# Layer norms of a four-layer block kernel: application and turn moved, their bank changed, constants loaded by another queue

## What is computed

```python
x = x + jnp.tanh(g_xattn[l]) * attention_l(_layernorm(x), ctx_4096, ...)
x = x + jnp.tanh(g_ffn[l]) * ffn_l(_layernorm(x), ...)

def _layernorm(x, axis=-1, eps=1e-05):
    m = jnp.mean(x, axis=axis, keepdims=True)
    v = jnp.var(x, axis=axis, keepdims=True)
    return (x - m) / jnp.sqrt(v + eps)
```

## Time and profile before

| | us |
|---|---|
| median of 3 runs | 2834.5 |
| lowest and highest | 2828.12 and 2834.67 |
| profiled execution, its own time | 2834.56 |
| its span in the trace | 2832.7 |
| PE busy | 2510.4 (89%) |
| DVE busy | 1857.0 (66%) |
| ACT busy | 1303.8 (46%) |
| POOL busy | 1286.5 (45%) |

### The profile page before, as it was taken

One profiled execution on the slowest core, in us unless ns is written; L12 is line 12 of the kernel. 1 busy time (PEld: TensorE's weight loads), 2 busy tenths in 40 slices (PEclk: granted clock), 3 DMA queues, 4 the chain that ended last, 5 costly groups with the idle time before them and its releaser, 6 DMA issues.

```text
span 2832.7 us, 42470 instructions
## 1 busy us (share of the span) xinstructions
PE 2510.4 (89%) x13827; PEld 2123.7 (75%) x13827; DVE 1857.0 (66%) x3455; ACT 1303.8 (46%) x3752; POOL 1286.5 (45%) x1423
## 2 busy tenths in 40 slices
PE   4899999997899999999978886878589999999865
PEld 3788888886778888888757775655468888888643
DVE  4777777767677777776757663522467777776765
ACT  2454545453245555555435443123145555555323
POOL 4554545543234444444436553334344444444245
PEclk7999999998899999999999997899799999999878
DMA  3111111111012222212000002269211111110047
GB/s 116 48 33 35 35 39 35 35 33 34 12 53 79 97 94 88 69 35 68 31 8 8 5 10 66 67 227 303 67 34 48 34 38 34 36 33 12 8 161 255
DMA packets 69102, 178.95 MB, mean 63 GB/s; under 512 B 10515, under 2 KB 11217, under 8 KB 66682
## 3 DMA queue, kind: packets, MB, share of 16 engines
q1 hardware_dynamic: 52048, 112.25, 12.3%
q0 software_dynamic: 13632, 61.10, 6.5%
q10 hardware_dynamic: 3210, 2.89, 0.3%
HBM read 157.84 MB, written 37.25 MB: 69 GB/s over the span
## 4 chain that ended last, share of the span: by engine, by line
PE 74%; DVE 8%; DMA 6%; issue 5%; POOL 5%; ACT 3%; ACTq 0%; POOLq 0%; SPq 0%; DVEq 0%
PE B_qkv L670 28%; PE B_out L670 19%; PE B_oT L741 4%; PE B_s L721 4%; PE B_qT L711 3%; PE B_oT L670 3%; PE B_pt L731 2%; PE B_s L722 1%; DMA raw<-in_experts,tables 1%; DMA raw<-slots_y,tables 1%; PE B_s L670 1%; PE B_oT L808 1%; PE B_qT L670 1%; POOL ring_l L1939 1%; PE B_qT L907 1%
## 5 line engine op out<-in xcount | busy, mean ns | idle before, releaser
L1179 ACT ACTIVATE W<-S,nmx 128x128 f32<-128x128 f32 x768 | 297.7, 394 | 58.2 <-DVE nmx L1469 58.2
L1947 POOL TENSOR_SCALAR rn<-ss 128x5 f32<-128x5 f32 x128 | 25.7, 201 | 621.5 <-DVE ss L1412 621.5
L1076 ACT ACTIVATE sq<-B_qkv 128x640 f32<-128x640 f32 x128 | 90.3, 706 | 423.7 <-PE B_qkv L670 423.7
L1968 POOL TENSOR_TENSOR S<-S,mask 128x512 f32<-128x512 f32 x192 | 251.5, 1310 | 17.0 <-ACT S L1019 16.9
L1487 DVE SCALAR_TENSOR_TENSOR X<-B_out,gates,X 128x512 f32<-128x512 f32 x200 | 150.1, 751 | 164.6 <-PE B_out L670 163.2
L2007 POOL TENSOR_TENSOR W<-W,rden 128x512 f32<-128x512 f32 x192 | 200.4, 1044 | 105.9 <-DVE rden L1474 105.8
L670 PE MATMUL B_qkv<-ring_h,xnT_h 128*128 128x512 f32 x512 | 216.3, 422 | 5.0 <-DVE xnT_l L1321 5.0
L670 PE MATMUL B_out<-ring_h,oT_h 128*128 128x512 f32 x516 | 209.6, 406 | 12.3 <-DVE kT L1459 8.6
L721 PE MATMUL B_s<-kT,qT_h 128*128 128x256 f32 x768 | 203.4, 342 | 11.0 <-DVE xnT_l L1321 9.8
L670 PE MATMUL B_out<-ring_l,oT_h 128*128 128x512 f32 x516 | 209.3, 406 | 0.1
L670 PE MATMUL B_out<-ring_h,oT_l 128*128 128x512 f32 x516 | 208.7, 404 | 0.0
(11 more groups left out here) (452 smaller groups left out, 8179.8 us busy)
## 6 DMA issues: line engine op xcount, KB each, us to landing
raw<-in_pieces SPq DMA_DIRECT2D x270, 256.0 KB
slots_y<-S SPq DMA_DIRECT2D x31, 256.0 KB
slots_y<-y SPq DMA_DIRECT2D x15, 256.0 KB, 8.2
X<-in_x ACTq DMA_DIRECT2D x8, 256.0 KB, 3.1
raw<-in_ctxT SPq DMA_DIRECT2D x8, 256.0 KB
rows_x<-xn SPq DMA_DIRECT2D x8, 256.0 KB, 2.0
out_x<-X SPq DMA_DIRECT2D x8, 256.0 KB, 3.3
raw<-in_quant SPq DMA_DIRECT2D x4, 256.0 KB
```

Of the source, the lines that this page charges most:

```text
L1179: t = act.activation(W[:, k, cols(r)], S[:, k, cols(r)], ACT.Exp, bias=nmx[:, k, r:r + 1], accum_out=den[:, k, r:r + 1])
L1968: pool.tensor_tensor(S3, S3, m.unsqueeze(1).to_broadcast([P, R, P]), ALU.add).then_inc(*masked.now((layer, u)))
```

## The change

norm spreads over two iterations: stats at place 12 of iteration i, apply at place 6 of i+1 (was 37 of i), turn at place 45 of i+1 for ffn0, ffn1 and ffn3 and at 33 for attention (was 7). The turns of the feed-forward stages go to bank B_oT instead of B_sc. The loads of X stand at iteration (b-2)//2: b=1 to 3 in iteration 0, 4 and 5 in 1, 6 and 7 in 2. The 12 small loads go from ACT to SP: gates in iteration 3, the other ten one at a time in iterations 14 to 23. The tanh stands in iteration 5 and DVE's make_constants in 28, both at place 57; the bias lands in the xn buffer instead of W.

```diff
-    def norm(self, i, stage, b, late=False):
+    def norm(self, i, stage, b):
         self.at(i, 12, "ln_stats", stage, b)
-        self.at(i, 37, "ln_apply", stage, b)
-        self.at(i + 1, 66 if late else 7, "ln_turn", stage, b)
+        self.at(i + 1, 6, "ln_apply", stage, b)
+        self.at(i + 1, 45 if stage.startswith("ffn") else 33, "ln_turn", stage, b)
...
         for b in range(1, NB):
-            self.at(max(0, b - 2), 1, "load_x", b)
+            self.at(max(0, (b - 2) // 2), 1, "load_x", b)
...
-        self.at(1, 2, "late_constants")
-        self.at(2, 5, "make_constants")
+        for n in range(CONSTANTS):
+            self.at(3 if n < 2 else 12 + n, 1, "load_constant", n)
+        self.at(5, 57, "make_gates")
+        self.at(16 + CONSTANTS, 57, "make_constants")
...
-            return (B_qT, "qT") if (stage, b) in plan.between or stage in ("attn0", "attn1", "attn3") else (B_sc, "sc")
+            return (B_qT, "qT") if (stage, b) in plan.between or stage in ("attn0", "attn1", "attn3") else (B_oT[:, :], "oT")
...
-            def make_constants():
+            def make_gates():
                 act.wait_ge(*small["g_xattn"].of(0))
                 act.wait_ge(*small["g_ffn"].of(0))
                 act.activation(gates[:, :], gates[:, :], ACT.Tanh).then_inc(*tanhed.now(0))
-                W_reader[0] = const.of("bias_hi"), const.of("bias_lo")
...
-                biases = W[0:LO_ROW + E3 + 1, 0, :]
+                biases = xn[0:LO_ROW + E3 + 1, 0, :]
...
+            def load_constant(n):
+                name, dst, src = (("g_xattn", gates[:, 0:4], io["g_xattn"].partition_broadcast(P)),
...
+                if name == "bias":
+                    for b in range(NB - 2, NB):
+                        sync.wait_ge(*ln_turned.of(("attn0", b)))
+                sync.dma_start(dst, src).then_inc(*small[name].now(0))
```

More of the change, by code:

```diff
@@ L42 @@
 VSLOTS = 6
+CONSTANTS = 12
 CHUNKS = NB * 2 * R
@@ L1025, in load_small @@
                 act.dma_start(dst, src).then_inc(*small[name].now(0))
-            def rows(vec):
-                return vec.partition_broadcast(P)
             def prologue():
@@ L1309, in scalar_program @@
             parts = {"project2": project2, "turn_q2": turn_q2, "exp2": exp2, "turn_p2": turn_p2, "oT2": copy_o2,
-                     "load_x": load_x, "late_constants": late_constants, "make_constants": make_constants, "ln_turn": ln_turn,
+                     "load_x": load_x, "make_gates": make_gates, "ln_turn": ln_turn,
                      "split": split, "project": project, "turn_q": turn_q, "split_k": split_k, "scores": scores, "low_scores": low_scores, "exp": exp, "turn_p": turn_p, "times_v": times_v, "low": low,
@@ L2138, in load @@
                     sync.dma_start(raw[:, k, :], io["pieces"][row][:, part]).then_inc(*landed[k].now(i))
+            def load_constant(n):
+                name, dst, src = (("g_xattn", gates[:, 0:4], io["g_xattn"].partition_broadcast(P)),
+                                  ("g_ffn", gates[:, 4:8], io["g_ffn"].partition_broadcast(P)),
+                                  ("bias", xn[0:LO_ROW + E3 + 1, 0, :], io["bias"]),
+                                  ("mask13", mask13[:, :], io["mask13"]),
+                                  ("mask2", mask2u[:, :].bitcast(I32), io["mask2"]),
+                                  *((f"norm_w{k}", norm_w[:, k:k + 1], io["norm_w"][k]) for k in range(4)),
+                                  ("groupmask", groupmask[:, :], io["groupmask"]),
+                                  ("gate_b", gate_b[:, :], io["gate_b"].partition_broadcast(P)),
+                                  ("rev", rev[:, :], io["rev"].partition_broadcast(P)))[n]
+                if name == "bias":
+                    for b in range(NB - 2, NB):
+                        sync.wait_ge(*ln_turned.of(("attn0", b)))
+                sync.dma_start(dst, src).then_inc(*small[name].now(0))
             def fill_tables():
@@ L2177, in tile3 @@
                 sync.dma_start(slots_y[t * P:(t + 1) * P, :], y3[:, t % 4, :]).then_inc(*y_stored[t % 4].now(t))
-            parts = {"load": load, "fill_tables": fill_tables, "clear_slots": clear_slots,
+            parts = {"load": load, "load_constant": load_constant, "fill_tables": fill_tables, "clear_slots": clear_slots,
                      "keep_rows2": keep_rows2, "fill_dispatch2": fill_dispatch2, "turn_ids2": turn_ids2, "contract2": contract2,
```

## The result

| | before | after |
|---|---|---|
| median, us | 2832.2 (4 runs) | 2922.2 (4 runs) |
| lowest and highest | 2828.12 and 2834.67 | 2918.37 and 2926.24 |
| span of the profiled execution | 2832.7 | 2920.8 |
| mean granted clock | 0.945 | 0.925 |

The change costs 90 us: ratio 1.0319, 95% interval 1.0299 to 1.0340. The forecast was 2902, the range 2855 to 2932.

The account below looks back on a forecast made before the run. The prediction took PE, busy 89% of the span, as the bound, so its waits are mostly paid in full. From 2834.6 us, +62.3 of waits and +5 of slower clock gave 2902, range 2855 to 2932.

Parts of the forecast that it names:

- The sum of the waits: All stages: the start's gain and the later turns' waits on PE, together +62.3 us.
- Start: said -3: Kernel start: ACT's 12 load issues go, so the first copies and turn_q come sooner; -3 us, bounds -6 and +2.
- ffn0 and attn1 together: said 32.4: Iterations 64 to 75: xnT_l comes later and PE waits for it; +23.6 us for ffn0, +8.8 for 72 to 75.
- ffn1: said 7.5: ffn1's iterations: the product waits for the later turn, copy and xnT_l; +7.5 us, bounds 2 and 14.
- attn3: said 6.6: attn3: first projection and last two turns later, other turns absorbed by additions of gathered rows; +6.6 us, bounds 2 and 14.
- ffn3: said 18.8: ffn3: the turn waits for the bias addition in B_oT, so route3 starts later; +18.8 us, bounds 8 and 26.
- The clock: PE's granted clock, lowered by more waits: 24 us possible in ffn0, ffn3 and ffn1, only 5 taken.
- rival (a): ffn0, ffn1 and ffn3: the full 24 us of slower clock comes due, giving 2921 us; chance 0.16.
- (b): All iterations: DVE sets the pace; freed of 46.3 us of waits it has xnT_l ready in time, 2812 us; chance 0.08.
- (c): Waits swap one for one, as in attn3: 2834 us, the same time; chance 0.04.
- (d): Half the bank waits are covered by work the forecast put in series: 2850 us; chance 0.08.
- The +14: Some 15 steady iterations would pay 0.95 us each if applications met POOL's work at the new place; left to the range.

Follow-up runs that it names:

- turn_mid: Kernel before with the change's start and the turn moved to place 33 (attention) and 36 (ffn), application left at 37, old banks: ratio 1.0207, 2887.8 us.
- const_only: Kernel before with only the small constant loads moved to SyncE one at a time and finished later, X loads as before: 2827.4 us, ratio 0.9994.
- the filling: The whole change plus unread small matmuls while PE waits, ahead of turns in ffn0 and ffn1 and of ffn1's products, in two bank versions: 2931.7 and 2930.4 us.
- apply_late: Kernel before with the change's start and the application at place 55 of its old iteration instead of 37, turns at 7: 2823.1 us, ratio 0.9974.
- start_only: Kernel before with only the change's start (constant loads and earlier X loads), norms and banks as before: 2825.3 us, ratio 0.9975.
- apply_only: Kernel before with the change's start and the application at place 6 of the next iteration, turn still at 7, old banks: ratio 1.0213.
- turn36_sc: The whole change, but ffn turns at place 36 in bank B_sc instead of 45 in B_oT: ratio 1.0281.

## Why the prediction was right, and where it was not

**The mechanism and the size of the waits: right where they were counted singly.** Turn_q of iteration 74 was put at 4.86 us behind X's start and came at 4.73. In ffn0 the time from the last output product's end to the product in iterations 66 to 69 went from 5.92, 5.89, 5.61 and 6.33 us to 9.47, 8.93, 9.10 and 9.24: +3.6, +3.0, +3.5, +2.9, where 3.7, 3.3, 3.6 and 3.0 were said. (These times hold some work at the lower clock too, such as transposes.) In ffn1 it went up by 1.6 to 1.7 in iterations 133 to 136 (3.34 to 4.92 in 135), where 1.6 to 1.8 was said. But 132, put at none, became 1.6 us longer as well, and the last two, put at 0.5 together, lost 1.5 and 1.6 before their products: the count had left out waits there. At attn3's first projection +2.4 was said; PE's two waits ahead of it came to 18.7 us and had been 16.5, +2.2. turn_mid shows by itself that the late place of the turn is enough for a loss of 66 us.

**The sum of the waits: too high by 15.** Said +62.3, measured +46.9. Start: said -3, came -4.9 of waits and -5.3 of time; the twelve issues' 4.5 us is there (turn_q of the first unit at 33.65, was 38.00), and the earlier loads of X cost 0.8 us at most (137.1 against 136.3 in const_only). ACT and PE of after, against the earlier trace rows:

```profile
21.23 0.63 ACT L1022 ACTIVATE ctxT_h<-raw 128x512 fp32r<-128x512 f32 x1 [0.25 <-DMA raw<-in_ctxT]
...
27.31 0.63 ACT L1022 ACTIVATE ctxT_h<-raw 128x512 fp32r<-128x512 f32 x1 [1.46 <-DMA raw<-in_ctxT]
```

```profile
33.65 1.08 PE L714 MATMUL B_qT<-ident,qk 128*128 128x128 f32 x4 [1.50 <-DVE xnT_l L1308]
```

The copy that had 6.56 us of issue ahead of it, at 27.25, now comes at 21.23 and waits 0.25 us for its data. The two behind it wait 3.36 and 1.46 us for theirs, so data set them, as was said: the one at 27.31 stood at 31.92 before, 4.6 us later, and v's copy behind it at 32.45, now at 27.84. ffn0 and attn1 together: said 32.4, came 25.3. ffn1: said 7.5, came 10.5. attn3: said 6.6, came -0.6 of waits, with 4.4 of time over the whole stretch with the gathered rows. ffn3: said 18.8, came 16.1.

**The clock: the step that failed.** "ffn1 has 16% of idle time at 1.00 now, so I take only 5." The busy time grew by 41.2. The term was an eighth of what it should be; even rival (a), 24, had a good half. Rival (a) had its three stretches nearly right, 24 said and 27.4 come (ffn0 8.8, ffn1 8.6, ffn3 10.0), and had no price for the other 13.8, of which 7.0 lie in the rest of attn1. What misled: I read from ffn1's row that idle time need not lower the clock, and treated the share of idle time as the measure. The rows of one iteration show otherwise: ffn1 with one wait of 1.76 us ahead of the product keeps 1.00, and with 1.65 and 1.50, with 0.63 us of transposes between, it falls to 0.65 during the product. The Trainium skill ("TensorE: Matmul & The Clock Gate", What's actually happening) says that half rate is the default and activity releases it. The trace agrees in the four stretches where PE's busy share fell (ffn0 0.82 to 0.74, attn1 0.92 to 0.86, ffn1 0.84 to 0.78, ffn3 0.69 to 0.63): the level fell in each, now in ffn1 too. It does not account for the gathered rows with attn3's start and the end, where the busy share did not fall and the level still went from 0.89 to 0.87 and from 0.87 to 0.83. That longer matmuls are the clock is shown for ffn1 by the filling; for the rest of the 41.2 us it is read from PEclk, which fell in each of these stretches.

So the total of 2902 was 20 low as the net of two errors of opposite sign, +15 and -36; that it came so near was luck in part. Rival (a)'s 2921 agrees with the result by the same luck: its waits were too high and its clock too low.

**The rivals.** (b), that DVE's stalls decide, is refuted: DVE's wait for rstd fell from 46.3 us to 2.7, its queue still brought xnT_l later, and apply_late, which takes the application off the way of qT and kT, gains nothing in the end. (c) and (d) are too small by the result. The +14 for applications that meet POOL's work at their new place: one took 540 ns in the middle and 1541 at most, so the short duration that the sum used was right and the +14 did not come (against the earlier trace rows; the column is shortest, median, longest):

```profile
L1360 DVE TENSOR_SCALAR xn<-X,mv,rstd x60: 533/540/1541, 7.2 to 2773.5; 128x512 f32<-128x512 f32 x60
```

The Trainium skill ("SBUF — State Buffer", Who interferes with whom) says that VectorE and GpSimd share a pair of ports, that an instruction such as tensor_scalar can take both of VectorE's, and that the one that issues first then holds the pair while the other blocks. The trace agrees with it in the longest one, in iteration 75: it starts at 862.44 us, 0.01 us after one of POOL's, and takes 1.54 us. At the new place such meetings are rare.

**What was said to show it.** Turn_q for xnT_l 25 us or more in some 15 places: 31.4 in 18. B_oT products for xnT_l 25 or more: 19.9 in 14, with 29.9 in 14 more at the turn ahead of them, which the sum had inside it but the list had not named. The router's near 15: only 7.3 in 6. DVE's for rstd near 5: 2.7. The first turn_q at 33 to 34: 33.65. Scores for xnT_l gone: no such row after.

## What to carry to other kernels

When a step moves to a later place, write down what stands ahead of it in the queue of the engine that ends it, iteration by iteration; here that gave most single times in ffn0, ffn1 and attn1 within 0.4 us, and missed 1 to 2 us where a place was passed over as covered. Then price PE's slower clock apart from the waits, and not by one factor: against the kernel before, 47 us of new waits came with 41 us of longer matmuls, and against start_only the traces have 48.5 and 15.6 us in apply_only, 40.6 and 22.0 in turn_mid, 50.3 and 29.8 in turn36_sc, and 54.7 and 44.7 in the change. A busy time that grows at equal counts is the sign, and durations of single matmuls (0.39 and 0.63 us) show where. A stall taken off an engine that is not the bound (46 us here) may be worth nothing, while two places of one chain can each cost the same 66 us, so undoing either alone brings back little.

## What was not expected of the hardware

In one product of ffn1 the clock fell about 1 us after PE had taken up work again, and then stayed at the lower level for some 3 us of full work (1470.6 to 1473.6); in another it had fallen already in the waits (0.74 from 1479.0 to 1482.5). No wait of PE there was longer than 2.1 us. Ten small matmuls around the turn kept ffn1 at 0.99 where the change has 0.91. In ffn3 filling ahead of the bias product raised PEclk by only 0.02 at 0.75; why is open.
